# Two graph layers on one core: the index fetches on four semaphores, at most two under way before the next

## The reference, cut to what matters

```python
h = maximum(layernorm(x), 0)
agg = segment_sum(edge_attr_64, tgt) / maximum(counts, 1)      # tgt = edge_index[1] = dst
x = x + relu(concat([agg, h]) @ W1 + b1) @ W2 + b2             # 64 + 256 -> 512 -> 256
h = maximum(layernorm(x), 0)
summed = segment_sum(h[src], dst)
x = x + h @ w_self.T + b_self + (summed / maximum(deg, 1)) @ w_neigh.T
```

## Time and profile before

| what | value |
|---|---|
| median of 3 runs | 1301.45 us (1298.68 to 1305.99) |
| the profiled execution's own time | 1301.85 us |
| its span | 1300.0 us, 31,886 instructions |
| mean granted TensorE clock | 0.955 |
| PE busy (matmuls) | 1196.8 us, 92% |
| DVE, ACT, POOL busy | 804.3, 518.5, 416.7 us |

### The profile page before, as it was taken

The page is one execution under the profiler, slowest core; times in us unless marked ns, Lnnn a source line. Parts: engine busy times, 40 slices in busy tenths (PEclk is TensorE's granted clock), DMA queues, the critical chain, the costliest instruction groups (busy, mean ns, idle before and its releaser), DMA issues.

```text
span 1300.0 us, 31886 instructions
## 1 busy us (share of the span) xinstructions
PE 1196.8 (92%) x11694; PEld 933.4 (72%) x11694; DVE 804.3 (62%) x1738; ACT 518.5 (40%) x982; POOL 416.7 (32%) x384
## 2 busy tenths in 40 slices
PE   2879999999999857959999999999999999999997
PEld 1878888888888735846777776776776777777774
DVE  3556666665665343857676676666676775766762
ACT  3672232332232113444444444444444444444441
POOL 3001101010110572006445454453463463453451
PEclk9879999999999766969999999999999999999998
DMA  3985443444445110102112222122121121221221
GB/s 106 320 270 164 131 128 118 120 123 121 122 127 188 52 55 23 33 25 70 57 58 66 57 70 61 56 69 56 56 74 51 53 80 48 61 71 55 62 66 40
DMA packets 67034, 115.87 MB, mean 89 GB/s; under 512 B 10644, under 2 KB 30824, under 8 KB 66962
## 3 DMA queue, kind: packets, MB, share of 16 engines
q1 hardware_dynamic: 51922, 75.12, 18.7%
q0 software_dynamic: 15040, 39.80, 11.0%
HBM read 101.93 MB, written 12.95 MB: 88 GB/s over the span
## 4 chain that ended last, share of the span: by engine, by line
PE 81%; DVE 6%; issue 5%; DMA 3%; DVEq 2%; ACT 2%; another core or an unknown queue 1%; SPq 0%; ACTq 0%
PE bank L1070 32%; PE couples L882 13%; PE couples L1063 9%; PE bank L917 7%; PE bank L1089 7%; PE bank L907 5%; PE bank L905 3%; DVE hids L1510 2%; DMA kreg<-in_edge_attr_dram 2%; PE bank L1081 1%; PE bank L1101 1%; DMA hreg<-in_dst_dram 1%; PE couples L874 1%; PE couples L907 1%; DMA xr<-in_x_dram 1%
## 5 line engine op out<-in xcount | busy, mean ns | idle before, releaser
L1070 PE MATMUL bank<-hreg,areg 128*128 128x512 f16 x2058 | 504.6, 382 | 0.0
L583 POOL DMA_INDIRECT wide<-h_table,aggn x280 | 324.5, 1159 | 450.6 <-PE couples L1063 281.3
L1510 DVE TENSOR_TENSOR hids<-iota,kreg 128x1024 bf16<-128x1024 f16 (+1 forms) x672 | 388.3, 626 | 94.1 <-PE couples L1063 92.7
L769 ACT ACTIVATE areg<-couples 128x784 bf16<-128x784 f32 x336 | 276.9, 824 | 371.8 <-PE couples L1063 370.2
L1070 PEld LDWEIGHTS bank<-hreg,areg 128*128 128x128 bf16 x2058 | 265.5, 144 | 104.6 <-issue 1.1
L882 PEld LDWEIGHTS couples<-oreg,kreg 128*64 128x64 f32 x3232 | 206.2, 144 | 40.7 <-issue 32.0
L882 PE MATMUL couples<-oreg,kreg 128*64 128x48 f32 x3232 | 218.0, 228 | 16.0 <-DMA kreg<-in_edge_attr_dram 7.5
L1063 PEld LDWEIGHTS couples<-hids 128*128 128x128 bf16 x2688 | 156.5, 99 | 71.9 <-issue 11.6
L883 PE MATMUL couples<-oreg,ones 128*64 128x48 bf16 x1616 | 199.3, 213 | 0.0
L1063 PE MATMUL couples<-hids 128*128 128x98 bf16 x2688 | 179.5, 209 | 11.1 <-DVE hids L1510 11.1
L883 PEld LDWEIGHTS couples<-oreg,ones 128*64 128x64 bf16 x1616 | 167.4, 109 | 0.0
(11 more groups left out here) (159 smaller groups left out, 963.6 us busy)
## 6 DMA issues: line engine op xcount, KB each, us to landing
kreg<-in_edge_attr_dram SPq DMA_DIRECT2D x202, 256.0 KB, 3.0
h_table<-hreg SPq DMA_DIRECT2D x25, 256.0 KB
xr<-in_x_dram SPq DMA_DIRECT2D x6, 1024.0 KB, 7.3
out_dram<-hbuf SPq DMA_DIRECT2D x42, 128.0 KB
wide<-h_table,aggn POOLq DMA_INDIRECT x280
wide<-in_L_gnn_W_dram SPq DMA_DIRECT2D x2, 512.0 KB, 6.6
out_dram<-h0buf SPq DMA_DIRECT2D x6, 128.0 KB
hreg<-in_dst_dram SPq DMA_DIRECT2D x1, 512.0 KB
```

Source lines behind the costliest of these rows:

```text
L583: pool.indirect_dma_start(near[:, k, :], None, table, bass.IndirectOffsetOnAxis(ap=nearsrc[:, n * GHALF + k:n * GHALF + k + 1], axis=0)).t ...
L769: act.activation(step.rearrange("p (a k) -> p a k", a=2), cpl[s % 2][:, :, 0:BC * KEYS], ACT.Copy).then_inc(s_adj, 1)
L1070: ins = pe.matmul(bank[4 + par], adj[:, par, :, h], htab[:, h, :], start=(h == 0), stop=(h == TN - 1))
L1510: ins = dve.tensor_tensor(o[:, q, :, :].rearrange("p c (v d) -> p c v d", d=2), iota16[:, 0:size].rearrange("p (v d) -> p v d", d=2).unsqu ...
```

## The change

- `s_places` becomes four semaphores, `s_places_0` to `s_places_3` (`LANES` = 4). Fetch j (0 to 41) adds its 16 to semaphore j mod 4.
- Before fetch j, from j = 3 on, POOL waits until fetch j - 3 has landed, by that fetch's own semaphore. So a fetch is issued once at most two are under way.
- The two waits after blocks of 14 go. After the 42nd fetch POOL waits for all four semaphores, ahead of the `s_near` fetches.
- DVE's `keys(n)` waits for four counts instead of one.

```diff
+        def landed(n, lane):
+
+            return 16 * (-(-(n - lane) // LANES))
...
             for b in range(DB):
                 for k, v in enumerate((dst, src)):
+                    j = 2 * b + k
+
+                    if j > 2:
+                        pool.wait_ge(s_places[(j - 3) % LANES], landed(j - 2, (j - 3) % LANES))
                     pool.indirect_dma_start(kreg[:, k, b, :], None, v.rearrange("(e a) -> e a", a=1),
-                                            bass.IndirectOffsetOnAxis(ap=startu[:, b:b + 1], axis=0)).then_inc(s_places, 16)
-                if b % KB == KB - 1:
-                    pool.wait_ge(s_places, 16 * 2 * (b + 1))
+                                            bass.IndirectOffsetOnAxis(ap=startu[:, b:b + 1], axis=0)
+                                            ).then_inc(s_places[j % LANES], 16)
+            for lane in range(LANES):
+                pool.wait_ge(s_places[lane], landed(2 * DB, lane))
...
             def keys(n):
                 frm = kreg[:, 1, bass.ds(n * KB, KB), :].rearrange("p b s -> p (b s)")
-                dve.wait_ge(s_places, 16 * 2 * KB * (n + 1))
+                for lane in range(LANES):
+                    dve.wait_ge(s_places[lane], landed(2 * KB * (n + 1), lane))
```

More of the change, by code:

```diff
@@ L91, in gnn_kernel @@
     CYCLE = 6
+    LANES = 4
     GW = 32
@@ L278, in gnn_kernel @@
         s_start = sem("s_start")
-        s_places = sem("s_places")
+        s_places = sems("s_places_", LANES)
         s_keys = sem("s_keys")
```

## The result

The changed kernel takes **1312.18 us** (median of 9 runs, 1308.68 to 1316.21), the one before 1301.45 us in the 9 runs beside them. The ratio is 1.0087, with a 95% interval of 1.0066 to 1.0108: slower by 0.9%, or 10.7 us. The forecast was 1301 us with a range up to 1312, so the time lies just outside. What came is the first rival, which had 1310 us and a chance of 0.17.

A forecast was written before the change was run, and what follows sets the result against it. PE was taken as the bound, with 40.6 us lost beside POOL's fetches. Stall end -2.5, lost pauses +2.0 and DVE's waits +0.3 summed to -0.2 us: 1301.65 profiled, 1301 us median, range 1290 to 1312.

The forecast's parts named there:

- the first rival: POOL's fetch stretch: the pauses kept PE going, so removing them is slower, 1310 us; chance 0.17.
- Where the time could come from: First two layer steps, beside POOL's fetches: PE's signals come late and 40.6 us are lost, about 3% of the kernel.
- The pauses' removal: POOL's two waits between blocks: dropping them saves 2.9 us, and POOL's burst ends 2.5 us earlier overall.
- The 39 waits: POOL, before fetches: each wait is met 1.1 us before POOL reaches it; together they cost 0 to 0.4 us.
- The margin: POOL's new waits: landing takes at most 3.44 us beside slow fetches, still under the 3.75 us of three distances.
- DVE's waits: DVE's three `keys` calls: nine more waits cost between 0 and 0.8 us, taken as 0.3.
- The stall: PE beside POOL's fetches: ends 2.5 us earlier with the burst, but each lost pause costs +1.0 us.
- Rival 1: POOL's fetch stretch: pauses kept PE going; +5.6 to +13.6 us, taken as +9, 1310 us; chance 0.17.
- The case against: Objection to the pauses keeping PE going: PE made 16 matmuls in 5.82 us from 452.11, in the middle of a block.
- The second argument: POOL and PE: if what they share is simply full, the sum of work is the same and pauses give nothing.
- The last argument: Objection to the pauses keeping PE going: POOL's total is the same with or without them.
- Rival 2: POOL's fetches: the limit holds POOL back or spread semaphores free PE; half gives 1281 us, all 1261; chance 0.12.

The follow-up runs named there:

- e3: Changed kernel, but before fetch j POOL waits for fetch j - 2 instead of j - 3: 1265.22 us, ratio 0.9718 to the kernel before.
- e12: e1 with a memset of six columns after each fetch, on the chip without the stall: 1264.05 us, ratio 1.0017 to the kernel before.
- e13: Kernel before with one memset in each of the first two pauses, on the chip without the stall: 1262.31 us, ratio 0.9985.
- e16: e3 run again in another job, on a second chip with the stall: 1271.16 us, ratio 0.9773 to the kernel before.
- e1: Changed kernel without the 39 waits, with three semaphores, one per block of 14, and still no pauses: 1315.40 us, ratio 1.0109 to the kernel before.
- e2: Changed kernel without the 39 waits, with pauses after blocks of 14 back, each waiting on all four semaphores: 1286.18 us, ratio 0.9877 to the kernel before.
- e4: Changed kernel, but before fetch j POOL waits for fetch j - 1 instead of j - 3: 1325.56 us, ratio 1.0169 to the kernel before.
- e7: e1 with a drain of POOL after each fetch: 1339.87 us, ratio 1.0269 to the kernel before.
- e8: e1 with a drain of POOL and a memset after each fetch: 1343.57 us, ratio 1.0280 to the kernel before.
- e6: Kernel before, with one semaphore, but POOL pauses for all landed after every four fetches: 1278.82 us, ratio 0.9790 to the kernel before.
- e5: Kernel before with three already met waits on one other semaphore added in each pause: 1305.38 us, ratio 1.0013 to the kernel before.
- e9: Kernel before with three already met waits on three other semaphores added in each pause: 1307.05 us, ratio 0.9998 to the kernel before.
- e10: e1 with two already met waits on other semaphores before each fetch: 1320.58 us, ratio 1.0136 to the kernel before.
- e11: e1 with four already met waits before each fetch: 1312.98 us, ratio 1.0060 to the kernel before.
- e17: e2 with only one wait in each pause, for the block's last fetch, on another chip: 1300.98 us, ratio 0.9991 to the kernel before.

## Why the prediction was wrong

**Where the time could come from: right.** The stretch of the fetches was named, with its late signals, and 40.6 us as what is lost in it. e3 gave back 38 of them, and the third stage kept its 725 us.

**The pauses' removal: right in size.** POOL's burst was to end 2.5 us earlier; it became 3.9 us shorter. The two pauses are 2.9 us of it, as forecast. Some 1.5 us of that is slow fetches beside DVE's `keys(0)` (1.71 us at 480.05) which the changed kernel does not have, as `keys(0)` there comes after the burst; the longer last wait takes 0.6 us back.

**The 39 waits cost 0 to 0.4 us and never hold: right,** within the 0.01 us of a distance, but in part by luck. "At most two under way" was true before the change; the limit was one fetch too loose, and e3, one tighter, holds. The margin, though, rested on a landing of at most 3.44 us beside `keys`, which I had read from how long POOL's instruction takes (1.71 us) and not from a landing. Where the traces have every landing's records (e12, e13), a fetch lands 2.4 to 2.8 us after its start, and beside `keys` up to 3.93, over the 3.75 of the waits. The changed kernel escaped that only because its `keys(0)` came after the burst. The rule of the Trainium skill ("SBUF — State Buffer", "A bandwidth-pool intuition that's wrong") weighed there speaks of 2.5 us more beside a copy on DVE; here it is 1.3 us more at most in e12 and e13. In e3 and e16 POOL went on from three waits only 5.07, 5.34 and 5.96 us after the start of the fetch that it waited for. Table writes ran beside these fetches and so did short operations of DVE; which of them held the fetch up is not shown.

**DVE's waits: 0.3 us, not testable,** since e1 has one wait per call and the same stretch within 1 us.

**The stall: this is the step that failed.** I wrote that without a pause "some 5.5 matmuls are left for later, at 0.19 us each: +1.0 us" for each pause, and set it against -2.5 for the earlier end. Two things were wrong in it. The pace between pauses was taken as given at 2.14 us per matmul, and a pause as a gain of a few matmuls. The runs show that the pace behind a pause depends on it: 36 matmuls in 13.6 us with the first pause and 22 without, 14 and 6 in the next 13 us, down to one per 2.80 us. The first addition is 40 us late instead of 10. For each pause I had put down 5.5 matmuls. And what is left was priced in matmuls, not in the chain that hangs on them: the late addition holds `keys(0)` behind it, which started 22 us ahead of POOL's last fetch before and 10 us behind it after. Rival 1 had that chain in it, with +5.6 and +13.6 as its ends and +9 as its price; measured are +10.7, with PE at 6 matmuls in the thirteen microseconds from 463.6, under the half of 15 that I had given as its condition. Part of the evidence for it stood in my own text, as PE's burst right behind a pause. The other part, ACT's release 0.6 us after the first pause, was a coincidence: ACT starts 19.7 us after the first fetch in both kernels (451.13 - 431.44, 452.77 - 433.04), with a pause ahead of it or without. The case against, PE's 16 matmuls in mid-block at 452, only showed that PE runs on before it is held; it does so in the changed kernel too (453.75).

The second argument, that a shared resource which is simply full gives the same end wherever POOL stops, falls with e3: 8 us of added idle time in pieces, in place of 2.9 in two pauses, return 38. In e2 1.2 us more in the pauses went with 16. The last argument, "its total is the same", was true of the bytes and beside the point.

**Rival 2** (the limit holds POOL back and PE is free) described e3, not this change. Its price of 40 us was right, and so was its condition, that the limit would have to hold.

## What to carry to other kernels

If signals of one engine come late beside a dense burst of indirect DMAs from POOL, the pauses in that burst may be what keeps the engine alive: before taking a wait out, ask what runs only while POOL is idle. A wait for the transfer k places back holds only where landing takes longer than k distances of issue. Here landing took 2.4 to 2.8 us: k = 3 (3.75 us) never held, k = 2 (2.5 us) held at half of the fetches. A trace tells that before the run, if the landing is read where it is slowest, beside the other engines' work. And time such a change on more than one chip: here it cost 0.9% in two jobs and a tighter limit gained 2.3 to 2.8%, while on one chip the stall that they deal with was not there at all.

## What the runs showed that I had not expected

- The stall depends on the chip. The kernel before took 1299.7 to 1304.3 us in six jobs, on at least four chips, and 1263.57 us in one; e12's fetches there were 1.25 us apart, as elsewhere. The changed kernel itself was not run on the chip without the stall; e1 to e3 neither.
- The traces do differ between these chips, in how many of their own records they keep. The 42 fetches of places add 42 x 16 = 672 times to their semaphores. e12 and e13, on the chip without the stall, have a record of all 672. The kernel before has 160, the changed one 150, and e4, e7 and e8, with fetches 2.9 to 3.4 us apart, all 672. In the view of DMA issues the time to landing (2.6 us) therefore stands for e13 and is missing for before:

```profile
kreg<-in_src_dram,startu POOLq DMA_INDIRECT x21, 2.6
...
kreg<-in_src_dram,startu POOLq DMA_INDIRECT x21
```

- Missing records are not the stall itself. e3 has 289 of the 672 and e6 420, with next to no late signal; and of the 4,480 increments of the third stage's gathers before has 3,387 and e13 all, yet that stage takes 725 us in both.
- Waits that are met beforehand cost POOL nothing, two to four of them, in its pauses (e5, e9) or ahead of indirect DMAs 1.25 us apart (e10, and e11 but for its three longer distances). With four waits in place of one a pause lasted 3.3 us in place of 2.7 (e2).
- A drain of POOL behind an indirect DMA holds it for about 2.4 us (e7): the next fetch starts 3.4 us after the last one, 0.9 us after its landing at 2.5 us.
- What PE and POOL share is still open. It is not DMA bandwidth (16% busy), not the semaphore (e17), and not a number of four fetches in a row as such (e6). Late are PE's signals and then PE, while ACT follows DVE at once (in the changed kernel DVE's operation ends at 491.37 and ACT starts at 491.40, in the midst of the stall). One candidate is the path that records events, which is short of records just on the chips with the stall. By the Trainium skill ("NOTIFIC — the notification-queue block", "Overflow: three behaviours, one of which stalls the engine") a record queue that is full can, in one of its settings, hold up the engine that writes to it. No run here shows that this happens, and none tried to. If it does, the stall may belong to executions that are recorded; no run compares them with others.
